# A graph network layer pair on one core: x turned once, the own term added at h0's eviction, and layer norm folded into the u product

## The chip, the core and the metric

The kernel runs on one core of one Trainium2 chip. The metric is the time of one execution in device microseconds (us). One execution was profiled as well; its span runs from the first to the last instruction.

## What is computed

1250 nodes with 512 features, 20,000 edges in both directions plus 1250 self loops, the edges sorted by `dst`:

```python
def _L0_gnn_ref(x, edge_index, eps, W1, b1, g1, be1, W2, b2, g2, be2):
    agg = segment_sum(x[src], dst, num_segments=N)
    h = (1.0 + eps) * x + agg
    h = relu(batch_norm(h @ W1 + b1, g1, be1))      # 512 -> 1024
    h = relu(batch_norm(h @ W2 + b2, g2, be2))      # 1024 -> 512
    return x + h

def _L1_gnn_ref(x, edge_index, W1, b1, W2, b2):
    h = relu(x @ W1 + b1) @ W2 + b2                 # 512 -> 256 -> 512
    agg = segment_sum(h[col], row, num_segments=N)
    return h + agg

x = layernorm(x + _L0_gnn_ref(x, ...))
x = layernorm(x + _L1_gnn_ref(x, ...))
```

`batch_norm` takes its statistics over the nodes, `layernorm` over the features. Everything is fp32.

## The kernel before

**Precision.** Products in fp32 are made from fp32r parts: each operand is split in a high part (a copy to fp32r, on ScalarE, "ACT") and a low part (operand minus high part, on VectorE, "DVE", or GpSimd, "POOL"), and TensorE ("PE") adds high by high, high by low and low by high in PSUM. A product with the adjacency counts needs only the two parts of the other operand.

**Sizes.** 1250 nodes are `NT` = 10 row tiles of 128 (the last has 98 rows); 512 features are `DT` = 4 blocks, 1024 hidden ones `HT` = 8, 256 are `LT` = 2. `CH` cuts the nodes in three column chunks 0 to 249, 250 to 749 and 750 to 1249. PSUM has 8 banks of 512 fp32 columns.

**Order of the work.**

1. *Edges.* The sorted edges are packed to pairs, written to DRAM and gathered in windows of ten destination nodes (two halves, L364). DVE makes them relative (`rel`, L664), counts those out of range (L668, L670), PE transposes them, DVE writes `keyT` and `loT`.
2. *Adjacency in 25 groups (slots).* For group `g` DVE writes one-hot matrices (`one_hots`, L683 and L686, two buffers), PE multiplies them (`build`, L923) and ACT copies the counts to 50 columns of `AT` (L443). After group 1 every engine branches on a flag (bad edge list or not).
3. *Aggregation, h0 transposed.* Item `i` = 4 c + d is feature block d of chunk c; it takes bank 2 + i % 6. `own(i)` (L886 to L894) adds (1 + eps) x with fp32 matmuls of x by a scaled identity `diag`; `aggregate(i, k)` (L927 to L944) adds two matmuls for row tile k. Chunk 0 is computed in slots 5 to 14, chunk 1 in 15 to 24, four of its 40 units per slot after the slot's build; chunk 2 comes after the branch. Items end one after the other: ACT writes the high part `h0h` (L462), DVE the low part `h0l` (L694). DVE also writes x's low parts `xl` (L653): four before the one-hots, one per group from group 2 on.
4. *First layer* (L993): eight times 36 matmuls, with batch norm by DVE statistics (L758) and ACT (L511, L513). Its weight is loaded whole (L302), split by blocks of input rows (L451, L375; POOL) in chunk 2, while ACT halves `AT` to int16 (`halve`, L485), DVE adds the identity (L779) and SP writes the tiles to DRAM (L307), from where they come back transposed (L323).
5. *Second layer* (L1006): 288 matmuls; the last two output blocks are computed in halves, and the last one ends chunk by chunk (`last_order`, `z_part`). The result `h2` is transposed, features on partitions. POOL widens the transposed adjacency (`A`, L409) from when the first half of `a1` was last used. x is loaded again into `xs`, over the second weight (L317).
6. *Tail, a pipeline over row tiles* (L1102 to L1114): `h2_rows` turns a tile of h2 back (L1043), DVE adds 2x (L801) and takes the statistics (L804), ACT the root (L547) and the normalised rows (L553); `x1_cols` turns these again (L1052), ACT and DVE split them (L563, L817); `hidden` multiplies by the weight, the bias being a matmul with ones (L1064, L1067); ACT applies relu and the high part (L572, L574), POOL the low part (L413); `own_and_neighbours` adds A times u in five banks (L1078, with 12 matmuls per tile, 5000 columns). `keep_warm` issues 14 matmuls without use (L1099) ahead of it.
7. *End*: five banks are split (L589, L842), the second product runs tile by tile (L1125), with layer norm by DVE (L848), ACT (L600, L603, L609) and POOL (L421), and SP stores (L327).

Each engine takes its instructions in the order written; semaphores order the engines among each other.

## Time and profile before

| | |
|---|---|
| runs, us | 284.90, 286.44, 287.74 |
| median | 286.44 |
| the profiled execution | 287.6 |
| its span | 285.8 |
| mean granted TensorE clock | 0.985 |
| TensorE matmuls | 259.5 us, 91% of the span |
| DVE | 144.4 us, 51% |
| ACT | 123.0 us, 43% |
| POOL | 76.6 us, 27% |
| the chain that ended last | PE 81%, DVE 7%, ACT 5%, DMA 4%, issue 1% |
| HBM | 10.94 MB read, 5.92 MB written |

The busy times are read from the head of the profile's page. A busy engine is not yet a bound: the chain of waits, followed back from the last instruction, says which engine's work set the end at each moment, and the table by stage says how much room the others had there. Matmuls are pipelined, so that the chain's time for a run of matmuls is of more use than the duration of one.

### The profile page before, as it was taken

Reading aid. Unit: us, or ns where it says so; the run is one execution under the profiler, and the core shown is the slowest. Engines: PE = TensorE matmul, PEld = TensorE weight load, DVE = VectorE, ACT = ScalarE, POOL = GpSimd, SP = SyncE. Lnnn points to the kernel's source line nnn. Section 1 sums busy time; section 2 is a strip of 40 time slices with the busy share of each in tenths; the row PEclk is TensorE's granted clock in tenths of the full one; section 3 lists DMA queues with packets and bytes.
Section 4 is the critical chain, followed back from the end, with each engine's and each line's share of the span. In section 5 each row is a group of like instructions: output and inputs, shape, how many; then the busy total and the mean of one; then the engine's idle time right before and its main releaser. Section 6 shows DMA issues by size and latency. Waiting matters only on the chain.

```text
span 285.8 us, 4044 instructions
## 1 busy us (share of the span) xinstructions
PE 259.5 (91%) x1581; PEld 221.6 (78%) x1581; DVE 144.4 (51%) x348; ACT 123.0 (43%) x217; POOL 76.6 (27%) x73
## 2 busy tenths in 40 slices
PE   0657999998999999999999999999769999999991
PEld 0636998886888888888888888888649888888770
DVE  1588997552743144444443313004474545448884
ACT  1407353424867047555556220200445445342694
POOL 5420000000920006565656700048301211112120
PEclk9999999999999999999999999999986999999998
DMA  4276000000056810000003795009000000000044
GB/s 139 93 277 240 0 2 0 2 0 6 2 203 236 274 42 1 2 0 0 2 20 126 254 234 102 0 19 202 11 1 2 1 0 2 0 0 2 3 180 175
DMA packets 21846, 20.43 MB, mean 71 GB/s; under 512 B 13911, under 2 KB 14846, under 8 KB 21826
## 3 DMA queue, kind: packets, MB, share of 16 engines
q1 hardware_dynamic: 21320, 19.91, 22.8%
q8 instruction: 14, 0.23, 0.3%
q0 software_dynamic: 160, 0.13, 0.2%
q10 hardware_dynamic: 346, 0.10, 0.2%
q14 instruction: 6, 0.05, 0.1%
HBM read 10.94 MB, written 5.92 MB: 59 GB/s over the span
## 4 chain that ended last, share of the span: by engine, by line
PE 81%; DVE 7%; ACT 5%; DMA 4%; issue 1%; DVEq 0%; SPq 0%; POOLq 0%
PE ps L1006 19%; PE ps L993 19%; PE ps L941 17%; PE ps L1078 7%; PE ps L1067 6%; PE ps L893 3%; PE ps L923 2%; PE ps L1052 2%; DVE hot_s L683 2%; PE ps L1125 2%; DMA src_i<-in_src 2%; PE ps L1043 1%; DMA pairs<-pair 1%; DMA run<-pairs,start_i 1%; PE ps L1064 1%
## 5 line engine op out<-in xcount | busy, mean ns | idle before, releaser
L758 DVE BATCH_NORM_STATS2 stats<-ps 128x6 f32<-128x500 f32 (+1 forms) x36 | 21.6, 599 | 63.1 <-PE ps L1006 35.2
L941 PE MATMUL ps<-AT,xh 128*128 128x500 f32 (+1 forms) x120 | 45.2, 385 | 0.0
L941 PE MATMUL ps<-AT,xl 128*128 128x500 f32 (+1 forms) x120 | 42.8, 364 | 0.0
L993 PE MATMUL ps<-h0h,wh 128*128 128x500 f32 (+1 forms) x96 | 34.0, 354 | 0.0
L993 PE MATMUL ps<-h0h,wl 128*128 128x500 f32 (+1 forms) x96 | 33.8, 352 | 0.0
L993 PE MATMUL ps<-h0l,wh 128*128 128x500 f32 (+1 forms) x96 | 33.7, 351 | 0.0
L443 ACT ACTIVATE AT<-ps 128x500 fp32r<-128x500 f32 x25 | 14.8, 590 | 32.3 <-PE ps L923 32.3
L941 PEld LDWEIGHTS ps<-AT,xl 128*128 128x128 f32 x120 | 24.3, 202 | 2.5
L941 PEld LDWEIGHTS ps<-AT,xh 128*128 128x128 f32 x120 | 24.2, 202 | 2.5
L1006 PE MATMUL ps<-a1h,wl 128*128 128x500 f32 (+1 forms) x96 | 24.9, 354 | 0.0
L1006 PE MATMUL ps<-a1l,wh 128*128 128x500 f32 (+1 forms) x96 | 24.8, 354 | 0.0
L1006 PE MATMUL ps<-a1h,wh 128*128 128x500 f32 (+1 forms) x96 | 24.8, 353 | 0.0
L501 ACT ACTIVATE std<-mv,epsc 128x1 f32<-128x1 f32 x12 | 3.5, 296 | 48.9 <-DVE mv L759 48.9
L375 POOL TENSOR_TENSOR wl<-w1s,wh 128x1024 fp32r<-128x1024 f32 x4 | 9.6, 2434 | 54.8 <-ACT wh L451 54.8
L683 DVE TENSOR_TENSOR hot_s<-iota,loT 128x1280 bf16<-128x1280 bf16 x25 | 20.5, 821 | 6.8 <-PE ps L923 6.5
L383 POOL TENSOR_TENSOR wl<-w2s,wh 128x512 fp32r<-128x512 f32 x8 | 11.0, 1381 | 47.3 <-ACT wh L521 47.3
L413 POOL TENSOR_TENSOR ul<-u,uh 128x256 fp32r<-128x256 f32 (+1 forms) x10 | 7.8, 784 | 49.0 <-ACT uh L574 49.0
L993 PEld LDWEIGHTS ps<-h0h,wh 128*128 128x128 f32 x96 | 18.0, 188 | 2.7 <-ACT a L513 0.3
L993 PEld LDWEIGHTS ps<-h0l,wh 128*128 128x128 f32 x96 | 18.1, 188 | 2.6
L993 PEld LDWEIGHTS ps<-h0h,wl 128*128 128x128 f32 x96 | 18.0, 188 | 2.4
L893 PE MATMUL ps<-diag,xs 128*128 128x128 f32 (+5 forms) x96 | 16.9, 326 | 2.2 <-issue 1.2
L387 POOL TENSOR_TENSOR a1l<-a,a1h 128x1250 fp32r<-128x1250 f32 x7 | 18.7, 2676 | 0.0
(141 smaller groups left out, 528.8 us busy)
## 6 DMA issues: line engine op xcount, KB each, us to landing
turns<-half_out SPq DMA_DIRECT2D x10, 320.0 KB, 2.2
xs<-in_x SPq DMA_DIRECT2D x1, 2304.0 KB
out<-xs SPq DMA_DIRECT2D x9, 256.0 KB
w1s<-in_L_gnn_W SPq DMA_DIRECT2D x1, 2048.0 KB, 10.4
w2s<-in_L_gnn_W SPq DMA_DIRECT2D x1, 2048.0 KB, 8.3
xs<-in_x SPq DMA_DIRECT2D x1, 1280.0 KB, 7.9
xs<-in_x SPq DMA_DIRECT2D x1, 1024.0 KB
lws<-in_L_gnn_W SPq DMA_DIRECT2D x1, 512.0 KB, 3.6
```

The source lines that it names most:

```text
L375: nc.gpsimd.tensor_tensor(wl[:, :, d * P:d * P + P], w1s[:, d, :].rearrange("p (m c) -> p m c", c=P), wh[:, :, d * P:d * P + P].bitcast(F3 ...
L383: nc.gpsimd.tensor_tensor(wl[:, t, :], w2s[:, t, :], wh[:, t, :].bitcast(F32), ALU.subtract).then_inc(w2l_set, 1)
L387: nc.gpsimd.tensor_tensor(a1(a1l, t), a32[t % 2][:, :], a1(a1h, t).bitcast(F32), ALU.subtract).then_inc(a1l_set, 1)
L443: nc.scalar.activation(AT[:, :, g * WG * WIN:(g + 1) * WG * WIN].rearrange("p k (w d) -> p k w d", w=WG), ps[:, g % 2, 0:GCOLS].rearrange( ...
L683: nc.vector.tensor_tensor(hot_s[g % 2][:, :, :, :], iota2[:, None, :, :].broadcast_to([P, WG, P, 2]), loT[:, w, None, :].broadcast_to([P, ...
L758: link(nc.vector.bn_stats(stats[:, 6 * c:6 * c + 6], ps[:, zbank(t, c), 0:c1 - c0]))
L893: mm(ps[:, 2 + i % RING, a - c0:b - c0], xs[0:rows[k], k, d * P:d * P + P], diag[0:rows[k], a - P * k:b - P * k], start=(a == c0), stop=Fa ...
L941: last = mm(o, part[0:r, k, d * P:d * P + P], AT[0:r, k, c0:c1], start=False, stop=(k == NT - 1 and j == 1), skip_group_check=True)
L993: last = mm(ps[:, zbank(t, c), 0:c1 - c0], w[:, t, d * P:d * P + P], h[c][:, d, :], start=(d == 0 and j == 0), stop=(d == DT - 1 and j == 2))
L1006: return mm(ps[:, zbank(t, c), 0:c1 - c0], w[:, k, (t - HT) * P:(t - HT + 1) * P], a1(a, k)[:, c0:c1], start=(k == 0 and j == 0), stop=(k ...
L1067: last = mm(o, xt[:, k % 2, d * P:d * P + r], w[:, d, :], start=False, stop=(d == DT - 1 and j == 2))
L1078: return mm(ps[:, V0 + b, f + c0:f + c1], (uh, ul)[j][0:r, k, m * P:m * P + P], a_rows(k)[0:r, c0:c1], start=(k == 0 and j == 0 and v_firs ...
```

## The change

The parts, in the order of the kernel:

- **x turned once.** PE transposes each tile of x (`x_cols`), ACT writes it to `xT` (`x_turn`): tiles 0 to 4 before the adjacency, 5 and 6 after builds 3 and 4, 7 to 9 after slots 6, 7 and 11. `own` and `diag` are gone.
- **Own term in h0's eviction.** DVE adds (1 + eps) xT to the item's bank (`h0_own`, in PSUM) two slots after the item is done; the high part follows three slots after, the low part five. Chunk 0 runs through its four items tile by tile (k outside, d inside).
- **Late branch.** The branch stands behind group 4, x's second half and its high and low parts are spread over slots 5 to 13, one of the two range counts goes behind the first group.
- **First weight by column blocks.** It is loaded into `w1s` by output blocks once x's first tiles are used; ACT writes its high parts in slots 15 to 22, POOL the low parts in place once `AT` is complete. The second weight comes through a ring of four 256 KB buffers.
- **The sum in columns.** 2 xT + h2 is formed with features on partitions (`xp_sum`) and split there. x isn't loaded again. The second layer's blocks are computed one after the other, statistics after each.
- **Layer norm folded into the u product.** The weight `lw1` is centred over its rows (a reduction, a product with `mean_w`, a subtraction), so that the product of the raw sums needs only the row's 1/std as a scale: `u_scale` on DVE multiplies by it and adds the bias. `x1_cols`, its split and the bias matmuls are gone. Three quarters of the product (`hidden_early`) need no part of the last feature block.
- **Three row banks.** The rows are turned back into three banks in turn; statistics are read from there, and `ln_apply` writes x1 from there.
- **Neighbours by column chunks.** u times A runs in chunks of 512, 512 and 226 columns; the second products of tiles 0 to 3 come before the last chunk.
- `keep_warm` is gone; the second layer's small weight is loaded after the second layer, ahead of the transposes of tiles 4 to 9.

The diff, cut to its core:

```diff
             sp.wait_ge(runs_asked, 1)
...
-            sp.dma_start(w1s[:, :, :], w1.rearrange("(k p) n -> p k n", p=P)).then_inc(w1_in, 16)
...
+            sp.wait_ge(x_turned, X_UNDER_W1)
+            sp.wait_ge(xl_set, X_UNDER_W1)
+            sp.wait_ge(x_in2, 32)
+            for d in range(DT):
+                sp.dma_start(w1s[:, :, d * P:d * P + P], w1[d * P:d * P + P, :].rearrange("p (t c) -> p t c", c=P)
+                             ).then_inc(w1_in, 16)
...
-            sp.dma_start(xs[:, 0:NT - 1, :], x[0:full, :].rearrange("(t p) d -> p t d", p=P)).then_inc(x_again, 16)
-            sp.dma_start(xs[0:rows[-1], NT - 1, :], x[full:N, :]).then_inc(x_again, 16)
             for k in range(NT):
                 b = k % len(half_in)
+                if k == len(half_in):
+                    sp.wait_ge(z_sum, BT)
+                    sp.dma_start(lw2s[:, :, :], lw2.rearrange("(k p) n -> p k n", p=P)).then_inc(lw2_in, 16)
                 if k >= len(half_in):
                     sp.wait_ge(A_set, k - len(half_in) + 1)
                 sp.dma_start_transpose(half_in[b][:, :, :], turns[:, P * k:P * k + P]).then_inc(turned[b], 16)
...
+            AHEAD = 8
+            for k in range(AHEAD):
+                if k == len(half_in) + 2:
+                    pl.wait_ge(xpl_last, 2)
+                widen(k)
             for k in range(NT):
+                if k + AHEAD < NT:
+                    widen(k + AHEAD)
                 u_low(k)
...
+            def x_turn(k):
+                r = rows[k]
+                act.wait_ge(x_turned, k + 1)
+                nc.scalar.activation(xT[:, :, P * k:P * k + r],
+                                     ps[:, x_bank(k), :].rearrange("p (d c) -> p d c", c=P)[:, :, 0:r],
+                                     ACT.Copy).then_inc(xT_set, 1)
...
+            def h0_own(i):
+                c, d = divmod(i, DT)
+                c0, c1 = CH[c]
+                v.wait_ge(h0_sum, i + 1)
+                if i == 0:
+                    v.wait_ge(xT_set, NT)
+                o = ps[:, 2 + i % RING, 0:c1 - c0]
+                nc.vector.scalar_tensor_tensor(out=o, in0=xT[:, d, c0:c1], scalar=eps1[:, 0:1], in1=o,
+                                               op0=ALU.mult, op1=ALU.add).then_inc(h0_own_set, 1)
...
+            def xp_sum(d):
+                for j, (c0, c1) in enumerate(xp_parts(d)):
+                    v.wait_ge(act_set, 2 * (HT + d) + 2 + j)
+                    nc.vector.scalar_tensor_tensor(out=xT[:, d, c0:c1], in0=xT[:, d, c0:c1], scalar=2.0,
+                                                   in1=a32[0][:, c0:c1], op0=ALU.mult, op1=ALU.add).then_inc(xp_set, 1)
...
+            def u_scale(k):
+                r = rows[k]
+                v.wait_ge(u_sum, k // 2 + 1)
+                if k == 0:
+                    v.wait_ge(lb1_in, 16)
+                if k >= UR:
+                    v.wait_ge(ul_set, k - UR + 1)
+                nc.vector.scalar_tensor_tensor(out=u32[0:r, k % UR, :], in0=u_at(k), scalar=ln_r[0:r, k, 0:1],
+                                               in1=lb1_all[0:r, :], op0=ALU.mult, op1=ALU.add).then_inc(u32_set, 1)
...
-            def own(i, k0=0, k1=NT):
-                c, d = divmod(i, DT)
-                c0, c1 = CH[c]
-                if i >= RING:
-                    pe.wait_ge(h0l_set, i - RING + 1)
-                for k in range(max(k0, c0 // P), min(k1, cdiv(c1, P))):
-                    a, b = max(c0, P * k), min(c1, P * k + P)
-                    mm(ps[:, 2 + i % RING, a - c0:b - c0], xs[0:rows[k], k, d * P:d * P + P],
-                       diag[0:rows[k], a - P * k:b - P * k], start=(a == c0), stop=False, skip_group_check=True)
-
+            def x_cols(k):
+                r = rows[k]
+                pe.wait_ge(*((x_in, 16) if k < half else (x_in2, 32)))
+                if k >= half:
+                    pe.wait_ge(xT_set, max(half, k - 1))
+                for d in range(DT):
+                    last = nc.tensor.transpose(ps[:, x_bank(k), d * P:d * P + r], xs[0:r, k, d * P:d * P + P],
+                                               ident[0:r, 0:r])
+                last.then_inc(x_turned, 1)
...
             with pe.If(bad == 0):
-                for g in range(NG):
-                    if g >= 2:
-                        build(g)
-                    if g >= 2 and DT + g - 1 < RING:
-                        own(DT + g - 1, 0, half)
+                for g in range(EARLY, NG):
+                    build(g)
                     for u in slot_units[g]:
                         aggregate(*u)
+                    if g in cols_at:
+                        x_cols(cols_at[g])
...
+            for k in range(7):
+                hidden_early(k)
+            for k in range(3):
+                xp_rows(k)
+            hidden_last(0)
+            hidden_early(7)
+            xp_rows(3)
+            hidden_last(1)
+            hidden_early(8)
+            hidden_early(9)
+            xp_rows(4)
+            hidden_last(2)
+            xp_rows(5)
+            hidden_last(3)
+            xp_rows(6)
+            neighbours(0, 0)
+            neighbours(0, 1)
+            hidden_last(4)
+            for k in range(7, NT):
+                xp_rows(k)
+                neighbours(0, k - 5)
+            for k in range(NT - 5, NT):
+                neighbours(0, k)
+                if k > NT - 5:
+                    neighbours(1, 2 * (k - NT + 4))
+                    neighbours(1, 2 * (k - NT + 4) + 1)
+            for k in range(8, NT):
+                neighbours(1, k)
+            for k in range(TPC):
+                second(k)
+            for k in range(NT):
+                neighbours(2, k)
+            for k in range(TPC, NT):
+                second(k)
```

On PE `neighbours(0, 0)` waits for `u32_set` 4, since the first neighbours' banks hold the first four tiles of u; each `neighbours(0, k)` waits for `ul_set` and `A_set` k + 1; `xp_rows(k)` waits from tile 3 on for `x1_set` k - 2.

## Rows read from the trace of the kernel before

**Rows 1.** Table by stage: length, busy us (instructions) by engine, granted clock, DMA share, GB/s.

```profile
28.68:44.58 15.90, 15.90 (x186) 15.38 (x187) 14.82 (x28) 6.98 (x14) 0.00 (x0) 1.00 0.00 1
44.58:69.10 24.52, 24.52 (x208) 19.73 (x204) 11.69 (x21) 7.84 (x14) 0.00 (x0) 1.00 0.01 2
69.10:93.29 24.19, 22.95 (x123) 19.64 (x122) 12.79 (x18) 18.29 (x28) 9.84 (x8) 1.00 0.35 136
...
203.28:213.94 10.66, 6.62 (x35) 4.61 (x33) 7.44 (x21) 4.63 (x8) 2.40 (x2) 0.93 0.01 2
213.94:219.60 5.66, 5.66 (x23) 4.90 (x24) 2.42 (x6) 2.95 (x6) 0.73 (x1) 0.52 0.00 0
219.60:265.35 45.75, 45.56 (x288) 39.31 (x288) 25.57 (x55) 19.74 (x45) 7.11 (x9) 1.00 0.01 1
265.35:279.60 14.25, 14.25 (x60) 11.04 (x60) 11.39 (x46) 11.36 (x30) 3.08 (x4) 1.00 0.28 104
279.60:285.80 6.20, 0.07 (x1) 0.00 (x0) 2.60 (x10) 2.45 (x7) 0.00 (x0) 0.87 0.48 173
```

**Rows 2.** Chain of waits, start to chunk 0: start us, us, what.

```profile
16.76 0.69 DVE xl L653
...
19.16 0.82 DVE hot_s L683
...
21.48 0.54 DVEq L705
...
28.68 0.60 PE ps L923 x10
...
31.59 1.87 PE ps L941 x8
...
38.38 1.02 PE ps L941 x8
```

**Rows 3.** Chain of waits, chunk 1 to the second layer.

```profile
53.77 0.28 PE ps L923 x10
54.05 1.90 PE ps L941 x8
...
70.08 1.24 issue
...
71.67 4.59 PE ps L941 x20
...
93.29 54.86 PE ps L993 x288
148.15 55.04 PE ps L1006 x288
```

**Rows 4.** Chain of waits, one row tile of the tail's steady part.

```profile
223.84 0.44 PE ps L1052 x4
224.28 0.31 PE ps L1064
224.59 1.63 PE ps L1067 x12
...
226.65 2.31 PE ps L1078 x12
```

**Rows 5.** Groups by line and form: busy us, mean ns of one, idle before.

```profile
L409 POOL CAST A<-half_in 128x1250 fp32r<-128x1250 int16 x6 | 7.2, 1230 | 25.6 <-PE ps L1006 25.4 <-DMA half_in<-turns 0.2
...
L413 POOL TENSOR_TENSOR ul<-u,uh 128x256 fp32r<-128x256 f32 x9 | 6.7, 749 | 45.6 <-ACT uh L574 45.6
...
L804 DVE BATCH_NORM_STATS2 ln_s<-xs 128x6 f32<-128x512 f32 x9 | 6.3, 695 | 0.3
...
L694 DVE TENSOR_TENSOR h0l<-ps,h0h 128x500 fp32r<-128x500 f32 x8 | 5.4, 678 | 11.3 <-ACT h0h L462 11.3
```

**Rows 6.** Two lines of code: ns min/median/max; to landing in us.

```profile
L323 SPq DMA_TRANSPOSE half_in<-turns x6: 1259/1975/5697, 158.5 to 193.7; - x6
...
DMA to landing us min/median/max: 3.8/4.3/11.5
...
L779 DVE TENSOR_TENSOR half_out<-half_out,ident x10: 261/294/2494, 74.8 to 91.3; 128x128 int16<-128x128 int16 x9, 98x98 int16<-98x98 int16 x1
```

More of the change, by code:

```diff
@@ L465, in _ @@
                 x_high(k)
+            for k in range(half):
+                x_turn(k)
+            for g in range(EARLY):
+                group_out(g)
+                if g >= EARLY - 2:
+                    x_turn(half + g - (EARLY - 2))
             act.wait_ge(flag_set, 1)
@@ L907, in _, with count @@
                 nc.tensor.transpose(ps[:, c, 0:NW], rel[0:NW, c * RUN:(c + 1) * RUN], ident[0:NW, 0:NW]).then_inc(rel_T, 1)
-            pe.wait_ge(n_out_set, 1)
-            pe.wait_ge(par_set, 1)
-            pe.wait_ge(const, 5)
-            for j in range(2):
-                last = mm(ps[0:1, 2, 0:1], n_out[0:NW, j:j + 1], ones[0:NW, :], start=(j == 0), stop=(j == 1))
-            last.then_inc(counted, 1)
-            own(DT, 0, half)
+            def count():
+                pe.wait_ge(n_out_set, 2)
+                pe.wait_ge(par_set, 1)
+                pe.wait_ge(const, 5)
+                for j in range(2):
+                    last = mm(ps[0:1, 2, 0:1], n_out[0:NW, j:j + 1], ones[0:NW, :], start=(j == 0), stop=(j == 1))
+                last.then_inc(counted, 1)
             def build(g):
@@ L976, in _ @@
                 pe.wait_ge(AT_set, NG)
-                for i in range(RING):
-                    own(i, 0, half)
                 for u in units[0:(len(CH) - 1) * per]:
@@ L1056, in hidden @@
-            def hidden(k):
+                    for j, (w, a) in enumerate(((wh, a1h), (wl, a1h), (wh, a1l))):
+                        for c, (c0, c1) in enumerate(CH):
+                            last = mm(ps[:, zbank(t, c), 0:c1 - c0], w[:, k, (t - HT) * P:(t - HT + 1) * P],
+                                      a1(a, k)[:, c0:c1], start=(k == 0 and j == 0), stop=(k == HT - 1 and j == 2))
+                    if (t, k) == (BT - 1, HT // 2 - 1):
+                        last.then_inc(a1_first_used, 1)
@@ new lines, in _, with hidden @@
+                last.then_inc(z_sum, 1)
+                if t == HT + 1:
+                    pe.wait_ge(mean_set, 1)
+                    pe.wait_ge(lsum_set, 1)
+                    mm(ps[:, 0, 0:L], mean_w[:, :], u32[:, 0, :], start=True, stop=True).then_inc(lmean_set, 1)
+            def hidden(k, d):
+                r = rows[k]
+                for j, (x, w) in enumerate(((xph, lw1h), (xpl, lw1h), (xph, lw1l))):
+                    last = mm(u_at(k), x[:, d, P * k:P * k + r], w[:, d, :], start=(d == 0 and j == 0 and k % 2 == 0),
+                              stop=(d == DT - 1 and j == 2), skip_group_check=True)
+                return last
@@ new lines, in hidden_early, with hidden_last, xp_rows @@
+            def hidden_early(k):
+                if 2 * (k // 2) == 4:
+                    pe.wait_ge(act_set, 2 * BT - 2)
+                for d in range(DT - 1):
+                    hidden(k, d)
+            def hidden_last(j):
+                part = 0 if 2 * j + 2 <= XP_A else 1
+                pe.wait_ge(xpl_last, part + 1)
+                for k in (2 * j, 2 * j + 1):
+                    last = hidden(k, DT - 1)
+                last.then_inc(u_sum, 1)
+            def xp_rows(k):
+                r = rows[k]
+                if k <= 2:
+                    pe.wait_ge(act_set, 2 * BT - 1 + k)
+                    pe.wait_ge(xp_set, DT + (1 if k == 2 else 0))
+                if k >= 3:
+                    pe.wait_ge(x1_set, k - 2)
+                for d in range(DT):
+                    last = nc.tensor.transpose(ps[0:r, row_banks[k % 3], d * P:d * P + P], xT[:, d, P * k:P * k + r],
+                                               ident[:, :])
+                last.then_inc(rows_T, 1)
@@ new lines, in neighbours @@
+            def neighbours(i, k):
+                r = rows[k]
+                c0, c1 = VC[i]
+                if i == 0:
+                    pe.wait_ge(ul_set, k + 1)
+                    pe.wait_ge(A_set, k + 1)
+                if k == 0:
+                    pe.wait_ge(u32_set, min(NT, 2 * v_banks[i][1] + 2))
+                for m in range(LT):
+                    for j in range(2):
+                        last = mm(v_at(i, m), (uh, ul)[j][0:r, k, m * P:m * P + P], a_rows(k)[0:r, c0:c1],
+                                  start=(k == 0 and j == 0 and (m == 0 or v_banks[i][0] != v_banks[i][1])),
+                                  stop=(k == NT - 1 and j == 1), skip_group_check=True)
+                if k == NT - 1:
+                    last.then_inc(v_sum, 1)
```

681 lines of the change are left out of this document (327 added, 354 removed).

## The prediction

> **What bounds the kernel now.** I read the chain of waits first, from slot 5 to the end. The chain runs over TensorE almost without a break: chunks 0 to 2 of the aggregation from 28.68, the first layer 54.86 us, the second 55.04 us [rows 2, 3]. So until 203.28 a saving counts only if it takes matmuls off TensorE or lets it begin earlier; what DVE, ACT and POOL do there is hidden as long as each stays below its stretch. The table by stage says how near they are [rows 1]: DVE 14.82 of 15.90 us in chunk 0 (the nearest), ACT 18.29 of 24.19 in chunk 2. From 203.28 it is otherwise. The first 10.66 us hold only 6.62 us of TensorE work, part of it matmuls that keep the clock up; the granted clock then reads 0.52 for 5.66 us, the 1.2 GHz level, after an engine that was idle four tenths of the time. From 219.60 TensorE is full again to 265.35, then 14.25 us of second products and 6.20 us from its end to the last store. Five stretches: 10.66 + 5.66 + 45.75 + 14.25 + 6.20 = 82.5 us, against 203.3 before them.
>
> **1, the start.** The chain waits for DVE from the gather to slot 5. Before the first one-hot at 19.16 lies a low part of 0.69 us at 16.76 that the change moves in front of the gather, and of the two range counts (0.44 each) one moves behind the first group; how soon the second gather lands is not shown, so I take 0.9 us of the 1.1. Three more low parts lie between groups 2 and 5, 0.6 us each, and go to slots 7 to 13: 1.8. The moved count costs 0.45, and the branch (0.54 us and two smaller pieces from 21.48, 0.9 in all) stays, now behind group 4 [rows 2]. Slot 5 begins at 28.68 - 0.9 - 1.8 + 0.45 = 26.4: **-2.3** (bounds -1.4 and -2.7). The turning of x's first five tiles, twenty transposes, lies in the wait for the gather; of the other five tiles two turn while TensorE waits for DVE.
>
> **2, chunk 0.** Its ten slots lose nothing: the own term's matmuls of tiles 0 to 4 were issued while TensorE waited for DVE, none lies in this stretch. Added are three turned tiles, four transposes each, 0.44 us at the high level [rows 4], about twice that at the low one. The first three slots run at the low level (1.87 us for eight products against 1.02 [rows 2], though the column of the granted clock reads 1.00 there [rows 1]), so two tiles cost 0.88: **+2.2**. DVE must carry 1.07 us of one-hots per slot plus a low part of 0.68 in slots 7 and 10 to 13, against 1.30 us of TensorE. It may run a slot and a half ahead, which just covers four times 0.4 us: 0, with 1.5 as the upper end. The four 250-column results now end together in slot 14; their additions, high and low parts have five slots.
>
> **3, chunks 1 and 2.** A slot without own term takes 0.28 + 1.90 = 2.18 us, ten of them 21.8 against 24.52: **-2.7**. Chunk 2 is four times 4.59 = 18.4 plus the 1.24 us that the chain calls issue, at the end of the branch; I let that stand: 19.6 against 24.19, **-4.6** (-5.8 if it goes) [rows 1, 3]. In return DVE adds the own term in PSUM, twelve instructions of at most 0.68 us, the row of the low part of the same width [rows 5]; DVE has 12.8 us idle in chunk 1 and 11.4 in chunk 2 [rows 1]. For the last result the way lengthens to own 0.68, high 0.59, low 0.68, some 2.1 us with the hand-overs, while the first layer has its first two column parts, over 4 us, to do. ACT writes the first weight's high parts in slots 15 to 22 instead of in chunk 2, which relieves its 18.29 us. POOL starts its eight low parts only at the end of chunk 1; eight at about 1.3 are 10.5 us of 19.6.
> One row there shows a lock: adding the identity takes DVE 0.29 us in the median and up to 2.49 beside a POOL subtraction [rows 6]. The Trainium skill, SBUF — State Buffer, "Who interferes with whom", has it that a DVE instruction with two SBUF inputs is held for the whole of a GpSimd one that reads SBUF; by that rule ten of these additions wait up to 1.3 us each here, which DVE's idle time holds, and the sum would be the same as by the row.
>
> **4, both layers.** 288 matmuls each before and after. The small product for the weight's mean, 256 columns in fp32, is not shown; its bounds are nothing and two passes like a 256-column product, 0.3: with its switch I take **+0.4**. The second layer's weight comes in a ring of four buffers; a buffer is needed again only four of the eight 6.86 us steps later. The second layer ends at 203.28 - 2.3 + 2.2 - 2.7 - 4.6 + 0.4 = 196.3; call it T.
>
> **5, the tail.** Now a tile costs TensorE 5.10 us: turned back 0.44 twice, bias 0.31, first product 1.63, neighbours 2.31 [rows 4]. One turn and the bias go: 5.10 - 0.44 - 0.31 = 4.35, ten tiles 43.5. Second products 14.1 and end 6.2 stay [rows 1]. Work 63.8.
> Is there a hole? At T TensorE has seven tiles of three quarters of the first product, 63 matmuls at 0.12 = 7.5 us. Under it run: three bank statistics (two wide of about 0.7 and 0.43; all now after T), coefficients 1.5, three rectifications 2, sum, high and low part 2.5: about 8.2. The first rows are turned at T+7.5. Then per tile DVE has statistics 0.70 [rows 5], small ones 0.55, scaling at most 0.42: with hand-overs 1.8, well under TensorE's 4.35. Two places wait: row tile 3 needs tile 0 normalised (statistics to x1, 3.9 us from T+7.9, TensorE there at 10.9): 0.9. The first neighbours' bank needs the fourth scaling: at T+19.1, TensorE there at 18.4: 0.7. POOL: the transposes for tiles 4 to 9 are issued only after T, one per 1.3 to 1.9 us, landing after 4.3; then eight widenings of 1.23 and a low part of 0.75 plus a maximum of half a microsecond [rows 5, 6]. Tile 4 lands at T+6, tile 8 at T+12.4, the first low part is done at T+15, four before it is wanted. Tail: 63.8 + 0.9 + 0.7 = 65.4 against 82.5: **-17.1**. The second products of tiles 0 to 3 before the last neighbours cost nothing and give ACT and DVE, 1.4 us a tile, a start.
>
> **The sum.** -2.3 + 2.2 - 2.7 - 4.6 + 0.4 - 17.1 = -24.1: span 285.8 to 261.7. The profiled execution took 287.6, 1.8 outside the span, and becomes 263.5; the median of the runs is 286.44 and becomes 262.3. I say 262.5.
>
> **Rivals.** *Other engines set the tail's pace* (0.22): a transpose behind loads took 11.5 us to land [rows 6], and the new weight load goes ahead of six of them; if tile 8 lands 7 us later the first low part comes at T+22, 3 us late, and each later tile waits on POOL's 2.5 us with little reserve: +3 to +7, 268. Against it: that load was 2.3 MB, this one 0.5. *The clock rises later in chunk 0, or drops after T* (0.12): each 1.3 us slot at the low level costs 1.0 more, all seven later slots +7; at T it takes waits as long as in the 10.66 us stretch: 269. For it: transposes take the place of matmuls early. *More than the sum* (0.13): the issue gap gone, the clock up two slots earlier since TensorE is full from 26.4, no hole in the tail: -1.2 - 2 - 1.6, 257.5. *The change does little* (0.03): if what I removed was filling waits that stay, chunks 1 and 2 keep their 7.3 us and the fill its 16 us: about 285. *Slower* (0.02): the low clock holds in the tail. TensorE has 57.6 us of work there; each microsecond of it done at 1.2 GHz costs one more, so it decides once more than 24.1, over two fifths, runs low; wholly low gives 320. Now 5.66 us were low, so it speaks against it that only long idleness brought it. My forecast has 0.48.
>
> **Numbers.** The forecast case with its own range is 259.5 to 265.5 (bounds of 1, DVE in 2, issue gap in 3). With the pace, clock and gain rivals the range is 256 to 270 and leaves out under 2 in 10. A measurement of this kernel tells about 1% from nothing: under 283.6 is faster, 0.95; within, 0.02; slower, 0.03.
>
> **What the new profile would show.** Slot 5's group at about 26.4; chunk 2 without own term, layer one at about 86; T near 196; no granted clock of 0.5 after T; first transposes of rows 7.5 us after T; TensorE over 95% busy from T to T+59. Wrong if: TensorE idle before the first neighbours with POOL as the releaser, one-hots late in slots 10 to 14, or layer one waiting for a low part.

## The result and the profile after

| | before | after |
|---|---|---|
| median of the runs side by side, us | 287.06 (284.90 to 287.74) | 263.36 (262.58 to 263.81) |
| the profiled execution, its span | 287.6, 285.8 | 263.5, 261.6 |
| mean granted TensorE clock | 0.985 | 0.972 |
| PE / DVE / ACT / POOL busy | 91 / 51 / 43 / 27% | 90 / 58 / 47 / 35% |

The ratio is 0.921, with a 95% interval of 0.917 to 0.925. The forecast was 262.5 and a span of 261.7. The number is right within 0.4%, but the part before the tail and the tail itself are each off by 6.5 us, in opposite directions. That they cancel is luck.

The table by stage of after answers to [rows 1]: length, busy us (instructions) of PE, PEld, DVE, ACT, POOL, granted clock, DMA share, GB/s. Its lines are chunk 0, chunk 1, chunk 2, the two layers, and from 189.65 on the tail.

```profile
24.21:39.27 15.06, 14.80 (x198) 14.18 (x196) 13.81 (x26) 10.43 (x19) 0.00 (x0) 0.97 0.36 97
39.27:61.05 21.78, 21.78 (x182) 17.02 (x179) 15.54 (x31) 12.54 (x25) 1.19 (x1) 1.00 0.01 3
61.05:79.26 18.21, 18.21 (x83) 15.08 (x82) 13.99 (x21) 13.75 (x23) 8.92 (x8) 1.00 0.38 145
79.26:134.23 54.97, 54.97 (x291) 47.20 (x290) 24.71 (x69) 28.23 (x40) 23.36 (x12) 1.00 0.16 51
134.23:189.65 55.42, 55.42 (x292) 47.86 (x292) 22.73 (x43) 14.43 (x19) 17.76 (x10) 1.00 0.16 34
189.65:197.50 7.85, 7.85 (x69) 7.85 (x69) 5.51 (x12) 3.52 (x6) 3.53 (x3) 1.00 1.00 165
197.50:201.90 4.40, 2.88 (x24) 2.46 (x22) 4.24 (x11) 1.40 (x4) 3.36 (x3) 1.00 1.08 211
...
212.40:221.50 9.10, 4.83 (x24) 3.25 (x22) 8.20 (x23) 5.92 (x13) 7.39 (x7) 0.90 0.00 0
221.50:237.00 15.50, 15.48 (x57) 12.52 (x58) 3.04 (x5) 1.09 (x2) 6.97 (x7) 0.84 0.00 0
```

The two stretches of the old tail with 10.66 and 5.66 us are gone, but a new one of 9.10 us has only 4.83 us of TensorE work, and behind it the granted clock has a mean of 0.84 over 15.50 us. That is 5.0 us at the lower of the two levels. The 56 products behind the gap take 15.48 us in the chain, and 13.25 in the first experiment below, where the level stays up: 2.2 us of time.

| place | forecast | measured | error |
|---|---|---|---|
| slot 5 begins | 26.4 | 24.21 | -2.2 |
| chunk 0 takes | 18.1 | 15.06 | -3.0 |
| chunk 1 | 21.8 | 21.78 | 0 |
| chunk 2 | 19.6 | 18.21 | -1.4 |
| both layers | 110.4 | 110.39 | 0 |
| T, the tail's begin | 196.3 | 189.65 | -6.6 |
| tail | 65.4 | 71.95 | +6.5 |

The start: the chain of waits of after (start us, us, what), answering to [rows 2]. L740 and L743 write the one-hots, L1034 is a build, L1054 the eight products of a slot, L1005 turns a tile of x, L715 writes its low part.

```profile
16.61 0.83 DVE hot_s L740
...
23.29 0.92 PE ps L1005 x4
24.21 0.42 PE ps L1034 x10
24.63 1.27 PE ps L1054 x8
25.90 0.28 PE ps L1034 x10
26.18 1.02 PE ps L1054 x8
...
29.38 0.60 ACT xT L499
...
31.01 0.69 DVE xl L715
31.70 0.74 DVE hot_s L740
...
37.43 0.34 DVE hot_k L743
...
37.82 0.43 PE ps L1034 x10
```

Three things are to be seen. The first one-hot begins at 16.61 where it was 19.16. The flag's work no longer stands in the chain. And after three slots, at 29.36, the chain leaves TensorE and goes over ACT and DVE up to 37.77, with one slot's TensorE work behind it. DVE set the end of the chunk, but only just: TensorE was 98% busy and waited 0.2 us in all, so the two bounds lie side by side.

The tail: the chain of after around the hole (L452 and L454 are POOL's maximum and low part of one tile of u, L1179 the product with A), and what TensorE waited for from T on (us in total, times, longest us).

```profile
216.91 0.86 POOL u L452
217.84 3.64 POOL ul L454
221.52 1.65 PE ps L1179 x3
```

```profile
PE ps L1179 <- POOL ul L454: 4.3, 2, 3.8
PE ps L1165 <- ACT x L629: 1.8, 2, 1.5
PE ps L1179 <- DVE u L924: 0.5, 1, 0.5
```

The second and third line are the two holes of the forecast. The first is not in it: most of its 4.3 us is one wait of 3.8, for a subtraction of POOL that took 3.6 us.

### The profile page after: what moved, and what is told of

Its sections match the earlier page's. It is cut to its first block, busy times and chain, and to the rows that moved or that the text cites. A ratio compares the mean times of both kernels' runs of the same rounds, so it can differ in the third digit from the quotient of the medians.

```text
span 261.6 us, 3850 instructions
## 1 busy us (share of the span) xinstructions
PE 236.7 (90%) x1463; PEld 202.4 (77%) x1463; DVE 150.7 (58%) x360; ACT 123.0 (47%) x217; POOL 92.6 (35%) x84
## 4 chain that ended last, share of the span: by engine, by line
PE 76%; DVE 10%; ACT 6%; DMA 3%; POOL 2%; issue 1%; SPq 0%; DVEq 0%
PE ps L1127 21%; PE ps L1110 21%; PE ps L1054 16%; PE ps L1179 8%; DMA xs<-in_x 3%; PE ps L1005 3%; PE ps L1197 3%; DVE hot_s L740 2%; PE ps L1034 2%; ACT u L661 2%; POOL ul L454 1%; PE ps L1140 1%; DVE ln_s L907 1%; DVE hot_k L743 1%; DVE xl L715 1%; DVE xpl L901 1%
## 5 line engine op out<-in xcount | busy, mean ns | idle before, releaser
L1054 PE MATMUL ps<-AT,xh 128*128 128x500 f32 (+2 forms) x120 | 42.8, 368 | 0.0
L1054 PE MATMUL ps<-AT,xl 128*128 128x500 f32 (+2 forms) x120 | 41.0, 353 | 0.0
L1179 PE MATMUL ps<-A,uh 128*128 128x512 f32 (+3 forms) x60 | 22.3, 388 | 4.8 <-POOL ul L454 4.3
L416 POOL TENSOR_TENSOR wl<-w1s,wh 128x512 fp32r<-128x512 f32 x8 | 10.1, 1301 | 46.6 <-ACT AT L491 46.6
L1054 PEld LDWEIGHTS ps<-AT,xh 128*128 128x128 f32 (+1 forms) x120 | 22.8, 190 | 2.7
L1054 PEld LDWEIGHTS ps<-AT,xl 128*128 128x128 f32 (+1 forms) x120 | 22.8, 190 | 2.7
L1127 PE MATMUL ps<-a1h,wl 128*128 128x500 f32 (+1 forms) x96 | 23.5, 354 | 0.0
L1127 PE MATMUL ps<-a1l,wh 128*128 128x500 f32 (+1 forms) x96 | 23.5, 353 | 0.0
L740 DVE TENSOR_TENSOR hot_s<-iota,loT 128x1280 bf16<-128x1280 bf16 x25 | 20.5, 819 | 2.3 <-PE ps L1034 2.1
L1179 PE MATMUL ps<-A,ul 128*128 128x512 f32 (+3 forms) x60 | 21.5, 374 | 0.0
L433 POOL TENSOR_TENSOR xpl<-xT,xph 128x1250 fp32r<-128x1250 f32 x3 | 8.7, 2886 | 34.7 <-ACT xph L610 34.7
L1110 PEld LDWEIGHTS ps<-h0h,wh 128*128 128x128 f32 x96 | 18.1, 188 | 2.9 <-issue 0.4
```

What stands on the lines that cost most here:

```text
L416: nc.gpsimd.tensor_tensor(wl[:, t, :], w1s[:, t, :], wh[:, t, :].bitcast(F32), ALU.subtract).then_inc(w1l_set, 1)
L433: nc.gpsimd.tensor_tensor(xpl[:, d, :], xT[:, d, :], xph[:, d, :].bitcast(F32), ALU.subtract).then_inc(xpl_set, 1)
L740: nc.vector.tensor_tensor(hot_s[g % 2][:, :, :, :], iota2[:, None, :, :].broadcast_to([P, WG, P, 2]), loT[:, w, None, :].broadcast_to([P, ...
L1054: last = mm(o, part[0:r, k, d * P:d * P + P], AT[0:r, k, c0:c1], start=(k == 0 and j == 0), stop=(k == NT - 1 and j == 1))
L1110: last = mm(ps[:, zbank(t, c), 0:c1 - c0], w[:, t, d * P:d * P + P], h[c][:, d, :], start=(d == 0 and j == 0), stop=(d == DT - 1 and j == 2))
L1127: last = mm(ps[:, zbank(t, c), 0:c1 - c0], w[:, k, (t - HT) * P:(t - HT + 1) * P], a1(a, k)[:, c0:c1], start=(k == 0 and j == 0), stop=(k ...
```

## Experiments on the tail

**One subtraction of 3.6 us.** The rows of the two lines that ran at that moment (ns min/median/max, first and last start): POOL's low parts, and DVE's additions of the second bias (L941, `base`) in the window from 217 us on.

```profile
L454 POOL TENSOR_TENSOR ul<-u,uh x10: 726/733/3629, 205.3 to 225.6; 128x256 fp32r<-128x256 f32 x9, 98x256 fp32r<-98x256 f32 x1
```

```profile
L941 DVE SCALAR_TENSOR_TENSOR x<-b_all,deg,x x4: 741/744/744, 218.2 to 220.1; 128x512 f32<-128x512 f32 x4
```

Nine low parts took 0.73, the tenth, begun at 217.84, took 3.63. From 218.15 DVE ran four additions with two SBUF inputs back to back, 4 x 0.744 = 2.98 us, and 0.73 + 2.98 = 3.71. My theory: the two engines shared one way into SBUF and POOL got none of it until DVE's train was through; then the clock fell because TensorE was idle. The additions aren't needed until the second products, so they can wait for the last low part:

```diff
             v.wait_ge(b2_in, 16)
+            v.wait_ge(ul_set, NT)
             for k in range(TPC):
                 base(k)
```

> The four instructions that add the second bias to x1 (base, two SBUF inputs each) wait until POOL has written all low parts of u. Theory lock: in the changed kernel the low part of tile 6 took 3.63 us instead of 0.73 because those four held POOL off; moved, it takes 0.73, TensorE's gap before the neighbours of tile 6 shrinks from 3.8 to about 0.9 us, the granted clock doesn't fall after it (another 2.3 us), and the time goes from 263.4 to about 258. Rival, POOL is late by its own pace (0.85 + 0.73 us a tile plus widening): the gap and the time stay, 263.

Measured: 258.84 us (258.54 to 259.26), 4.5 less than after; ratio to before 0.905 (0.901 to 0.909). All ten low parts take their 0.73 again:

```profile
L454 POOL TENSOR_TENSOR ul<-u,uh x10: 725/738/745, 205.6 to 223.7; 128x256 fp32r<-128x256 f32 x9, 98x256 fp32r<-98x256 f32 x1
```

The wait for POOL fell from 4.3 to 1.4 us, and the granted clock reads 1.00 from 212 to 228 us, where it read 0.50 from 220 to 224 in after.

**Is it the second input, or any work of DVE?** In the place of the additions four bank statistics with one SBUF input of the same width, and the additions still late:

```diff
+            for k in range(TPC):
+                v.wait_ge(x1_set, k + 1)
+                link(nc.vector.bn_stats(stats[:, 0:6], x1[0:P, k, :]))
             v.wait_ge(ul_set, NT)
```

> As e1_base_late, but in the old place of the four additions stand four bank statistics over x1, of about the same length, that read one SBUF operand (results unused). Theory lock by two SBUF inputs: POOL's low parts stay at 0.73 us and the time is that of e1_base_late within 0.5 us, about 258. Rival, any dense DVE work on SBUF slows POOL: tile 6's low part takes over 3 us again and the time is about 263.

Measured: 258.98 us (258.27 to 259.71), the low parts 725/733/746 ns, though the statistics ran without a pause from 219.19 to 222.06, over two of them. Nothing is lost. The statistics differ from the additions in one more point, they write 6 columns and not 512. After's own trace speaks against the writing: the scalings of u (L924, one input in PSUM and one in SBUF, 128x256 written to SBUF) ran inside low parts at 208.49 and 210.00, which took 0.73 and 0.74. So it is the second SBUF input that holds POOL up.

**How much of the 4.5 us is the clock?** After as it is, with 14 matmuls without use in the hole:

```diff
             for k in range(NT - 5, NT):
+                if k == NT - 4:
+                    pe.wait_ge(x1_set, 8)
+                    for _ in range(14):
+                        mm(ps[:, 6, :], lw1h[:, 0, 0:P], lw1h[:, 0:2, :].rearrange("p a b -> p (a b)"),
+                           start=True, stop=True)
```

> The changed kernel with 14 matmuls without use put into TensorE's gap before the neighbours of tile 6; the gap itself and what causes it stay. Theory: of the 6.5 us that the tail was longer than forecast, 3.8 are waiting and 2.4 are neighbours done at 1.2 GHz after it; with the engine occupied in the gap the granted clock stays at 1.00 and the time falls by about 2.4, to 261.0. Rival, the clock falls for another reason than the empty engine: 263.4 and 0.5 in the column again.

Measured: 261.70 us (260.83 to 262.51), the granted clock 1.00 from 212 to 228. That is 1.7 us less than after by the medians and 1.2 by the spans, where 2.4 was expected; the intervals of the two ratios (0.910 to 0.920, and 0.917 to 0.925) overlap slightly. The traces say more when counted from T, the end of the second layer. T came at 190.6 here and in the first experiment, 1.0 later than in after, although the instructions up to there are the same: the first slots' products took 1.87 and 1.11 us there, and 1.27 and 1.02 in after. From T on after takes 71.95 us, this kernel 69.8 and the one with late additions 66.8. So the level is worth 2.2 us, close to what was expected, and the shorter waits for POOL 2.9.

**What the filling at T is worth.** The forecast's largest gain rested on 7.5 us of product work that needs no part of the last feature block. Here the first three row tiles are turned ahead of it, so that it begins only when the last block is complete (on top of the late additions):

```diff
-            for k in range(7):
-                hidden_early(k)
             for k in range(3):
                 xp_rows(k)
+            for k in range(7):
+                hidden_early(k)
```

> e1_base_late with the first three row transposes in front of the seven tiles of the first product that the change put there. Theory: that product covers batch norm and the sum of the last feature block; without it TensorE is empty for 6.2 us at the start of the tail, the granted clock falls to 0.5 for some microseconds (3 more), and about 1.5 of the later waits go: +7.7, about 266 against 258. Rival, the cover is worth little because the row pipeline starts 1 us earlier and was the slower part: within 1 us of e1_base_late.

Measured: 266.68 us (266.62 to 267.25), 7.8 above the kernel with late additions. Its table around T, which is 190.00 here:

```profile
189.65:196.00 6.35, 0.34 (x2) 0.00 (x0) 3.96 (x10) 2.17 (x4) 3.44 (x3) 0.75 0.82 185
196.00:200.00 4.00, 3.00 (x14) 3.03 (x15) 3.66 (x5) 1.34 (x2) 1.78 (x2) 0.50 1.56 234
200.00:204.00 4.00, 4.00 (x25) 4.00 (x24) 2.81 (x10) 2.44 (x5) 3.22 (x3) 0.62 0.63 103
```

TensorE waits 7.0 us for the last block's sum, and the granted clock is at the lower level for 7 of the 8 us from 196 on: the old tail's pattern [rows 1] is back. This term of the forecast holds.

**A smaller reordering.** With late additions, `hidden_last(1)` goes ahead of `xp_rows(3)`, and ACT writes `lw2h` after its row pipeline (in after it stands in the chain at 214.72 with 0.95 us, ahead of two tiles):

```diff
-                if s == half + 2:
+                if s == NT + 1:
                     act.wait_ge(lw2_in, 16)
...
-            xp_rows(3)
             hidden_last(1)
+            xp_rows(3)
```

> e1_base_late with two more moves: ACT writes the small weight's high part after the row pipeline, not amid it, and the last quarter of the first product of tiles 2 and 3 comes before row tile 3 is turned. Theory: TensorE's remaining waits in the tail are 1.5 us for row tile 3, 1.4 for POOL's low parts and 0.5 for the fourth scaling; 0.85 of the first and most of the second go: -2, to 256.8. Rival, the pipeline is bound by POOL's 1.6 us a tile and the waits only move: within 0.5 us of 258.8.

Measured: 257.70 us (257.25 to 258.12), ratio to before 0.902 (0.895 to 0.908): 1.1 less, not 2. The waits fell from 1.8, 1.4 and 0.5 us to 1.1, 0.9 and 0.5. From T on it takes 65.6 us, 1.2 less than with the late additions alone. It is the fastest of all.

## Experiments on the start and the chunks

**Turning x before or inside chunk 0.** In after, tiles 5 and 6 are turned before slot 5. Here they move into slots 5 and 6, and two others one or two slots later:

```diff
-        cols_at = {6: half + 2, 7: half + 3, 11: half + 4}
-        turn_at = {6: half + 2, 7: half + 3, 12: half + 4}
+        cols_at = {5: half, 6: half + 1, 7: half + 2, 8: half + 3, 11: half + 4}
+        turn_at = {6: half, 7: half + 1, 8: half + 2, 9: half + 3, 12: half + 4}
```

> The changed kernel with the two turned tiles 5 and 6 moved from between builds 3 and 5 to the ends of slots 5 and 6 (tiles 7 and 8 one slot later each). Theory: the granted clock rose at 24.9 us, ten earlier than in the kernel before, because those transposes kept TensorE occupied from 21.4 on; without them it is half empty until 23.5, rises some 4 us later, and four slots cost 1.0 more each, less 0.7 for slot 5 beginning earlier: +3, 266.5. Rival, what else was made denser (builds 1.1 us apart instead of 1.7) does it: clock as early, and the time 262.5 to 263.4.

Measured: 266.48 us (265.82 to 267.22), 3.1 more than after, as expected. The chain:

```profile
24.95 1.88 PE ps L1052 x8
...
28.09 1.55 PE ps L1052 x8
...
33.74 0.69 DVE xl L713
...
40.22 0.34 DVE hot_k L741
```

The eight products of the first two slots take 1.88 and 1.55 us, where in after they take 1.27 and 1.02: the level rises about two slots later. One of these slots can't be put down to the edit: the four traces with late additions, one input, useless matmuls in the hole and the smaller reordering, whose start is that of after, show 1.87 and 1.02 to 1.14 (the fifth, with the filling undone, 1.41 and 1.01). Slot 5 isn't earlier, although 1.8 us of TensorE work is gone before it, since DVE's work is now what it waits for, and the first one-hot begins 0.7 later here (17.35 for 16.61). In the next slots DVE's one-hots wait 2.8 us in all for TensorE's builds (0.6 in after), and from 32 us on the chain is again ACT's and DVE's, 2.8 us later (40.56 for 37.77). So the delay came from the level, the later copies and in part the start together, and this run doesn't divide it.

**The level alone, in the kernel before.** Nine matmuls of 256 columns without use between builds 1 and 5 of before:

```diff
             def build(g):
+                if g in (2, 3, 4, 5):
+                    occupy({2: 4, 3: 0, 4: 1, 5: 4}[g])
                 pe.wait_ge(hot, 2 * g + 2)
```

> The kernel before with nine matmuls of 256 columns without use between builds 1 and 5, where TensorE waits for one-hots; nothing else moved. Theory: the late clock was worth three slots at 1.0 us; with the engine full the granted level is high at slot 5, and the time falls by 2 to 3 (DVE, 1.67 us a slot with its low parts, takes part of it back), to about 283.5. Rival, the clock's rise doesn't depend on what the engine does there: the same time as before, 286.

Measured: 285.69 us (283.93 to 286.88), ratio 0.999 (0.996 to 1.003): a miss. The level did rise earlier, and this is what it ran into:

```profile
33.27 0.34 DVE hot_k L686
...
33.66 0.43 PE ps L931 x10
34.09 1.02 PE ps L949 x8
```

The same place in before, the end of its third slow slot and the beginning of slot 8:

```profile
33.90 1.60 PE ps L941 x8
35.50 0.27 PE ps L923 x10
```

The chain now is DVE's up to 33.61. Slots 5 to 7 took 1.87, 1.87 and 1.60 us for their products in before, about 1.0 each here. But slot 8 could not begin before DVE's one-hots for it: 33.66, only 1.8 earlier than before's 35.50. Chunk 1 begins at 42.90 instead of 44.58, 1.7 earlier, and T comes 1.8 earlier (201.49 for 203.28). The medians show nothing of it. The executions that were traced don't stand for the medians here: before's took 287.6 us, 2 above the median of the thirteen run beside this kernel.

**DVE's order alone, and both.** Before, with chunk 0 computed tile by tile, so that the low parts of tiles 4 to 9 need not stand in groups 2 to 7; then the same with the nine matmuls of the last experiment:

```diff
-        units = [(c * DT + d, k) for c in range(len(CH)) for d in range(DT) for k in range(NT)]
+        units = [(d, k) for k in range(NT) for d in range(DT)]
+        units += [(c * DT + d, k) for c in range(1, len(CH)) for d in range(DT) for k in range(NT)]
...
+            LOW_AT = {5: 4, 7: 5, 10: 6, 11: 7, 12: 8, 13: 9}
...
-                    if g >= EARLY and g - EARLY + SOON < NT:
-                        x_low(g - EARLY + SOON)
+                    if g in LOW_AT:
+                        x_low(LOW_AT[g])
```

> The kernel before with two parts of the change alone: chunk 0's units run tile by tile (four blocks of a row tile, then the next tile), and so x's low parts of tiles 4 to 9 move from groups 2 to 7 to groups 5, 7, 10, 11, 12 and 13. Theory A (the start was bound by DVE and by the low clock one after the other, and each hides the other's removal): slot 5 begins three low parts earlier, at 28.68 - 1.8 = 26.9, but its first slots still run at the low level (8 products 1.87 us), chunk 1 begins at 44.86 - 1.8 = 43.1, so 285.7 - 1.8 = 284. Rival B (DVE alone was the bound, the level follows when TensorE gets work): slot 5 at 26.9 and full speed within one slot, chunk 1 at 41.5, 282.5. Rival C (neither matters, something else sets chunk 0's end, such as ACT's copies or high parts that now end together in slot 14): within 1 us of 285.7.

> The same spread of the low parts together with the nine useless matmuls of e6_occupied between builds 1 and 5. Theory A: now both bounds are gone at once, slot 5 at about 27 and all ten slots at 1.30 us from the second one on, chunk 1 begins at about 40.3, 4.5 us earlier: 281.2, more than the two alone together (0 for the occupied TensorE, -1.8 for the spread). Rival B: no more than the spread alone, 282.5 in both. Rival C: within 1 us of 285.7.

Measured: 285.16 us (283.46 to 286.99), ratio 0.998 (0.994 to 1.003), and 282.37 us (281.81 to 283.30), ratio 0.990 (0.982 to 0.998). The chain of the first:

```profile
39.69 0.34 DVE hot_k L687
...
90.60 54.85 PE ps L995 x288
```

It goes over DVE without a gap from 22.48 to 40.03: thirteen pairs of one-hots at 1.07 and six low parts at 0.60 are 17.5 us. Chunk 1 begins at 41.55, 3.0 earlier than in before and where rival B had put it; with the useless matmuls it begins at 42.09, no earlier, against the 40.3 of theory A. So in before the chunk had two bounds close together, TensorE with three slow slots and DVE's total, and in this order DVE's total is the one. The first kernel isn't DVE's order alone, though: its products ran at the high level from the first slot on, with nothing added for it. The first layer begins at 90.60 and 90.63 in the two (before 93.29). Only the second one's time shows the gain. The time of the first is not above or below before's by more than 0.7%, which is rival C's number with rival B's trace; its ten runs spread over 3.5 us. The traces show one source of such spread: after T, the lower level lasts for about 6.8 us in before, 3.4 in the first of these kernels and not at all in the second, though the instructions there are the same. From T to the end they take 82.5, 81.0 and 79.7 us, so part of the second one's gain is this and not chunk 0.

**The own term alone.** Before without the own term's matmuls of chunks 1 and 2 (items 4 to 11; h0 then lacks (1 + eps) x there):

> The kernel before without the own term's matmuls for chunks 1 and 2; the term itself is left out there, so this is the price of the matmuls alone. Theory: 7.3 us of them lie on the chain, and the 1.24 us gap at the end of the branch stays; but ACT, which carries the first weight's high parts and the halving in chunk 2, then becomes late with the last high part and takes some 2 us back: -5 to -6, about 281. Rival, nothing else is near: -7.3, or -8.6 if the gap goes too, 277.5 to 279.

Measured: 280.51 us (279.29 to 281.55), ratio 0.981 (0.973 to 0.989). The chain at the border of chunks 1 and 2, and the table behind it:

```profile
66.32 0.60 ACT h0h L462
...
66.94 0.69 DVE h0l L694
67.63 0.36 issue
67.98 19.99 PE ps L940 x80
```

```profile
66.30:68.00 1.70, 0.02 (x1) 0.05 (x1) 0.99 (x4) 1.68 (x3) 0.07 (x1) 1.00 0.01 5
68.00:72.00 4.00, 4.00 (x12) 3.20 (x12) 2.36 (x2) 4.00 (x6) 4.00 (x2) 0.60 0.02 4
```

The first layer begins at 87.97, 5.3 earlier than before, where the forecast had put 7.3 us on the own term. The rest is at the border: TensorE idles 1.7 us there, 0.4 more than in before, and afterwards the lower level holds for 3.2 of the next 4 us and 0.2 of the four behind them, which costs 1.7. 5.3 + 0.4 + 1.7 = 7.4, so the term itself was right. The time expected for the run, about 281, was met, but not for the reason given: it isn't ACT late with the last high part that takes the 2 us back, since the first layer follows TensorE's products without a gap. The gap stands where the branch ends, as before's 1.24 us did [rows 3]; the trace names the low part of chunk 1's last item as its releaser, while the code there waits only for an earlier one. What makes it isn't told apart. In after TensorE waits for nothing in either chunk.

**Taking low parts off DVE.** If DVE's total bounds chunk 0, and POOL is idle there, POOL could write the low parts of tiles 5 to 9. The rule of the tail's hole speaks against it. On top of the fastest kernel:

```diff
+            pl.wait_ge(xl_set, half)
+            for k in range(half, NT):
+                pl.wait_ge(xh_set, k + 1)
+                nc.gpsimd.tensor_tensor(xl[0:rows[k], k, :], xs[0:rows[k], k, :],
+                                        xh[0:rows[k], k, :].bitcast(F32), ALU.subtract).then_inc(xl_set, 1)
...
-                    if g in low_at:
-                        x_low(low_at[g])
```

> e7_order with the low parts of x's tiles 5 to 9 written by POOL (idle there) instead of DVE: five subtractions of 128x512, about 1.38 us each on POOL, beside DVE's one-hots. DVE's work from its first one-hot (16.75) to the one-hots of group 14 falls from 15 x 1.07 + 4 x 0.60 and 0.69 = 19.1 us to 16.1. If DVE's total sets the end of chunk 0 and POOL's instructions do not disturb it, chunk 0 ends about 2 us sooner, where TensorE's own work becomes the bound: 257.7 - 2 = 255.7. If the two engines hold each other off there as base and ul did (one-hots and low parts both have two SBUF inputs), either five pairs of one-hots wait up to 1.3 us each or POOL's subtraction is stretched to 3 us and more and TensorE waits for the low part: no gain or a loss, 257.5 to 261.

Measured: 260.94 us (260.54 to 261.39), ratio 0.914 (0.910 to 0.918): 3.2 more than without it, the second of the two cases. The chain, and POOL's subtraction:

```profile
31.89 1.43 DVE hot_k L749
33.32 1.83 DVE hot_s L746
35.15 1.40 DVE hot_k L749
36.55 1.83 DVE hot_s L746
38.38 0.34 DVE hot_k L749
```

```profile
L416 POOL TENSOR_TENSOR xl<-xs,xh x5: 1460/1840/1862, 26.4 to 36.2; 128x512 fp32r<-128x512 f32 x4, 98x512 fp32r<-98x512 f32 x1
```

Four one-hot instructions of the chain grew by 1.1 us each, together 4.3, for three us of work taken off DVE (a fifth, at 27.08, grew as well but lay beside other work of TensorE), and POOL's grew too (1.38 us for that size elsewhere, 1.84 here). DVE's chain ends at 38.72, and without the move at 38.80, but here with the one-hots of group 13 and there with those of group 14: DVE is a whole group, 1.07 us, behind. TensorE waited 1.4 and 0.7 us for the one-hots of groups 12 and 13, and behind that the granted clock has a mean of 0.60 from 38.76 to 43.00, which is 3.4 us at the lower level and costs 1.7. The first layer begins at 83.00 for 80.29: 1.07 + 1.7 is the 2.7 between them.

## Why the prediction was right, and where it was wrong

**Step 1, the start** (forecast -2.3, measured -4.5): mis-sized. I took 0.9 of 1.1 us for the removed work ahead of the one-hots; the first one begins 2.55 earlier. The removed work gave its 1.0, and the second half's numbers were in time. The other 1.5 lies ahead of it, where the forecast had nothing: DVE begins with the first gathered numbers 1.1 earlier, and `rel` takes 0.28 us for 0.77. The first line is of before, the second of after:

```profile
14.75 0.77 DVE L664 TENSOR_SCALAR rel<-run,win_pair 125x128 f32<-125x128 f32 x1 [2.75 <-DMA run<-pairs,start_i]
13.65 0.28 DVE L725 TENSOR_SCALAR rel<-run,win_pair 125x128 f32<-125x128 f32 x1 [0.41 <-DMA run<-pairs,start_i]
```

Why the gather landed earlier wasn't tried and stays open. The branch, 0.9 us that "stays, now behind group 4", lies beside TensorE's turning of tiles 5 and 6 and costs nothing. Against that stand two turned tiles at 0.92 each in the chain, which I had put into DVE's waits.

**Step 2, chunk 0** (forecast +2.2, measured -0.8): the step that failed. It carried three slow slots of before, 2.9 us, over into after, and 0.88 for two slowly turned tiles. In after one slot was slow, with 1.27, and no tile of this stretch: 0.4 us in all. DVE's order, which I had listed with "0, with 1.5 as the upper end", cost what stands there, 0.2 us of waiting. But a higher level alone wouldn't have given the 3 us, as the occupied kernel showed: in before's order DVE's one-hots stop it after 1.7. Both had to go, and the change took both away. DVE's total says how near its bound is: from 16.61, fifteen pairs of one-hots (16.2), the moved count (0.3), five low parts (3.1) and 1.6 us between them, 0.6 of it waiting for ACT's copies and 0.6 for TensorE's builds, make 37.8, and slot 14 behind it 1.5: 39.3. In before chunk 1 began at 44.58. The two kernels with one part of this each gained 1.7 and 3.0 us in their traces. A part of the step is chance: in the traces with the same start chunk 1 begins between 39.27, after's, and 40.30.

**Step 3**: chunk 1 as forecast to 0.1. In chunk 2 the issue gap went, the case that I had kept as an upper bound, and with the own term alone taken out it had not; which part of the change closed it wasn't tried. That DVE's added work is hidden held: 15.54 of 21.78 and 13.99 of 18.21 us, though the additions took up to 0.74 us and not "at most 0.68". I had weighed the rule of the Trainium skill (SBUF — State Buffer, "Who interferes with whom": a DVE instruction with two SBUF inputs contends with a GpSimd instruction that reads SBUF) against the additions of the identity there, where DVE has room. That the two contend was right, the place wrong; and I had asked only how long DVE would be held, while at the tail's hole it was POOL.

**Step 4**: +0.4 as forecast (27.50 and 27.50 with the mean's product, 0.43, between).

**Step 5, the tail** (forecast 65.4, measured 71.95): the mechanism of the gain was right, and the experiment that undid the filling priced it within 0.1 us of what was expected. The work was 63.2 us for 63.8, the two holes 1.8 and 0.5 us for 0.9 and 0.7. The step that failed is the one on POOL. That the first low part is done before it is wanted held (T+16.4, wanted at T+19.5), but the forecast case stopped there: the later tiles were left to POOL's own durations, and nothing was asked of DVE instructions beside them. The waits for it took 4.3 us and the lower level after them 2.2, both put at nothing. The late additions took back 5.1 of these 6.5. The rival that let other engines set the tail's pace had the right engine with the wrong cause: the transposes were in time. The rival with the clock dropping had the right effect as a consequence.

So the forecast case holds in chunks 1 and 2 but for the gap, the layers and the filling. Its total holds because the "more than the sum" rival came true before T, with a start 2.2 us earlier than that rival had, and parts of two others behind it. Of its own signs, the one-hot late in slot 14 came, if by 0.2 us; the granted clock did read 0.50 after T, and TensorE was 89% busy from T to T+59 and not over 95%. The cause of the level's earlier rise stays open in part: it rose early with useful transposes (after) and with useless matmuls (occupied), later where the transposes were moved back, but also early in the spread kernel, whose first products took 0.28 each at 27.2 with no work added ahead of them.

## What to carry to other kernels

Look on DVE for instructions with two SBUF inputs beside POOL's, and give them a wait if they aren't urgent: one line was worth 4.5 us here. Where an engine feeds a stage for many slots, add up its total from its first instruction to the last it must deliver and compare that end with the bottleneck's, rather than asking slot by slot. When two kernels differ in one stage only, compare their traces from that stage's begin: here 1 us that came before T hid half of what an experiment behind T had gained. When the terms of a sum are checked against a trace, check each; the total can be right for wrong reasons.

## What the hardware showed that was not expected

- POOL's subtraction had begun 0.3 us before the first of DVE's four additions and still gave way to all four: 3.63 us for 0.73. DVE's additions took their usual 0.744 each. In chunk 0 it was mutual: DVE's one-hots 1.83 for 0.74, POOL's 1.84 for 1.38. And with late additions it was the other way round: POOL's split of the small weight (L467), begun 0.14 us before the first addition, took 2.39 (2.42 in after), and that addition 2.8 for 0.74. Which of the two is held these runs don't settle.

```profile
224.38 2.39 POOL L467 TENSOR_TENSOR lw2l<-lw2s,lw2h 128x1024 fp32r<-128x1024 f32 x1
L941 DVE SCALAR_TENSOR_TENSOR x<-b_all,deg,x x10: 741/742/2815, 224.5 to 234.3; 128x512 f32<-128x512 f32 x9, 98x512 f32<-98x512 f32 x1
```

- DVE work with one SBUF input beside the same subtraction cost nothing (a median of 733 ns with it, 738 without).
- The column of the granted clock read 1.00 in before's first slots, while eight products took 1.87 us instead of 1.02; in after it read 0.50 from 20 to 25 us, where they were as slow. Durations say more than the column there.
- In before without the own term, 1.7 us without work, after TensorE had been full for over 20 us, were followed by the lower level; the 1.24 us at the same place in before were not (granted clock 1.00 in that stretch [rows 1]), nor were 1.59 us in the spread kernel, whose next 20 products took 4.58 us as in before.
- The lower level after T came and went between kernels whose instructions there are the same: a mean of 0.57 and 0.58 over two stretches of 4 us in before, 1.00 throughout in the spread kernel with useless matmuls.
